# TensorE's four parts of a step in another order, the old maximum a step ahead on VectorE, and other signals for the gathers of Pool

## The chip, the cores and the metric

The kernel runs on one core of a Trainium2 chip. The metric is the device time of one launch in microseconds (us), the median of several launches. A profiled execution gives, beside its time, a record of every instruction of the five engines: TensorE (PE, its weight loads apart as PEld), VectorE (DVE), ScalarE (ACT), GpSimd (POOL) and SyncE (SP), which issues DMAs.

## What is computed

A graph of 6250 nodes with 64 channels and 200,000 edges, sorted by destination, goes through two graph layers. The change lies in the first one, an attention that is applied in two hops:

```
def agg(emb):
    a_input = jnp.concatenate([emb[head], emb[tail]], axis=-1)
    h = a_input @ fc_w.T + fc_b
    e = jnp.sum(h * rel_e, axis=-1)
    e = jnp.where(e > 0, e, LEAKY_SLOPE * e)
    m = jax.ops.segment_max(e, head, num_segments=N)
    ex = jnp.exp(e - m[head])
    denom = jax.ops.segment_sum(ex, head, num_segments=N)
    w = ex / denom[head]
    agg_emb = jax.ops.segment_sum(emb[tail] * w[:, None], head, num_segments=N)
    return agg_emb + emb
for _ in range(N_HOPS):        # N_HOPS = 2
    emb = agg(emb)
    emb = emb / jnp.maximum(jnp.sqrt(jnp.sum(emb * emb, axis=-1, keepdims=True)), EPS)
```

After it come a layer norm, a second layer (gather, matmul with a weight that a GRU cell makes, segment sum, relu) and another layer norm. None of that is touched.

## The kernel before

The edges of a hop are cut into groups of 512, four tiles of 128 edges, padded so that a group belongs to one block of nodes. A hop takes one step for each group (about 400 steps), and each group passes through nine stages, one stage a step: in step `i` an engine works on group `i`, on `i - 1`, up to `i - 8`. `pipelined` writes eight steps out (`u` is 0 to 7), and a hardware loop runs over these eights. At the edge of an eight TensorE and ScalarE load the block numbers of the next eight steps from SBUF into registers (L83).

What each engine does in step `i`, in the order of before:

- **TensorE**: `sums(i-7)` (L1553, the probability weighted sums of the gathered rows), `scores(i-2)` (L1540 and L1543, the products with the nodes' scores; the first three products on L1543 take a block number from a register), `spread(i-4)` (L1524, four transposes that lay the scores over all partitions), `turn_prob(i-6)` (L1532, four transposes of the probabilities), `gather(i-1)` (L1504, one product with zeros that opens `ps_t`, then L1515, ten matmul records that fetch rows near the diagonal out of SBUF by one-hot products). The sweep loop in `gather` runs once a step here. Each part ends with a semaphore: `summed`, `x_rdy`, `s_spread`, `p_turned`, `gathered`.
- **ScalarE**: `prob` (L1579, out of `ps_p` once `p_turned` is told), `prob_t` (L1584), `alpha` (L1586), `acc` (L1591), `rows<-ps_t` (L1599, once `gathered` is told; its signal is `kept`), `lower` (L1603). `ps_t` has one buffer: the next gather's L1504 waits for `kept`.
- **VectorE**: `m_old` (L1625), `x_sum` (L1633), `masked` with the new maximum `m_new` (L1642), `s_raw` (L1649), `hot_t` (L1654), `score` (L1660), `hot_near` (L1669, waits for `gathered` of two groups back), `block_sum` (L1677, waits for `summed`).
- **Pool**: for each group two indirect DMAs (L1486) that gather the far rows of the group's last two tiles from HBM into `rows`. The first waits for `summed` of the group that last held the slot, the second for `p_turned` of group `g - 7`.
- **SyncE**: two broadcast loads a step and one load of indices every four steps.

## Time and profile before

| | us |
|---|---|
| median of 3 runs (5886.37 to 5901.3) | 5893.11 |
| the profiled execution | 5902.71 |
| its span (first to last instruction) | 5900.9 |

The page's line of TensorE's busy tenths over 40 slices of the span reads 3666666199999999996799999999974666666664. The two stretches of nines are the two hops. The mean granted clock over the span is 0.846 of full speed. By queue, the hardware DMA queue q1 moved 799.51 MB and Pool's queue q0 147.90 MB.

How such rows are read: a row of the timeline has the start (us from the span's start), the duration, engine, line, operation, what it writes and reads, the number of merged records, and in brackets how long the engine was idle before it and who ended that. Ends of matmuls are modelled. A releaser "issue" means that the engine waited for nothing that the profile shows.

### The profile page before, as it was taken

The page shows a single profiled execution, that of the slowest core. Times are in us where ns is not written, and L with a number is a line of the kernel's source. Part 1 is how long each engine was busy: PE and PEld are TensorE (multiplying, and loading weights), DVE is VectorE, ACT ScalarE, POOL GpSimd, SP SyncE. Part 2 cuts the span into 40 slices and gives each one's busy share as a digit, 9 for nine tenths or more (in the row PEclk, how much of TensorE's full clock was granted, in tenths as well). Part 3 has the DMA queues.
Part 4 walks back from the last instruction along what each step waited for, and adds up shares of the span by engine and source line. Part 5 has one row for each costly group of instructions (what it writes and reads, how often), then busy time and mean ns, then how long its engine had stood idle before and what let it go on. Part 6 is the DMA issues. An engine that isn't in the chain of part 4 may idle for free. (4 is left out here: it accounts for less than half of the span.)

```text
span 5900.9 us, 199689 instructions
## 1 busy us (share of the span) xinstructions
PE 4518.9 (77%) x53517; PEld 3713.5 (63%) x53518; DVE 3763.9 (64%) x11123; ACT 2406.1 (41%) x5659; POOL 2851.1 (48%) x2835
## 2 busy tenths in 40 slices
PE   3666666199999999996799999999974666666664
PEld 0001111098899898986798989999973555555553
DVE  8984887377777777777577777777773333333334
ACT  6201000066666666664466666666650111111111
POOL 0155666245555555552455555555532555555553
PEclk7668887599999999998899999999985766666666
DMA  7999999355555555553555555555531222222221
GB/s 284 404 413 410 413 415 415 109 146 144 145 150 145 145 150 146 144 149 69 143 150 147 146 148 147 148 147 149 147 84 42 50 50 50 50 49 51 50 50 39
DMA packets 489464, 949.05 MB, mean 161 GB/s; under 512 B 146548, under 2 KB 295693, under 8 KB 440209
## 3 DMA queue, kind: packets, MB, share of 16 engines
q1 hardware_dynamic: 397953, 799.51, 41.9%
q0 software_dynamic: 90336, 147.90, 11.2%
q8 instruction: 60, 0.98, 0.1%
q10 hardware_dynamic: 1072, 0.31, 0.0%
q14 instruction: 43, 0.35, 0.0%
HBM read 930.99 MB, written 14.32 MB: 160 GB/s over the span
## 5 line engine op out<-in xcount | busy, mean ns | idle before, releaser
L1486 POOL DMA_INDIRECT rows<-tab_d,stage_idx x1632 | 1611.4, 987 | 1620.2 <-PE ps_p L1532 592.7
L1515 PE MATMUL ps_t<-tab,hot_near 128*128 x8160 | 1146.7, 287 | 55.8 <-issue 27.4
L1868 POOL DMA_INDIRECT tab<-y_d,stage_src x768 | 727.7, 947 | 735.3 <-PE ps_all L1909 276.2
L1515 PEld LDWEIGHTS ps_t<-tab,hot_near 128*128 128x128 f32 x8160 | 1006.5, 193 | 105.5 <-issue 91.5
L1553 PE MATMUL ps_g<-rows,prob 128*128 128x65 f32 x6528 | 846.6, 273 | 171.1 <-issue 97.0
L1553 PEld LDWEIGHTS ps_g<-rows,prob 128*128 128x128 f32 x6528 | 793.8, 192 | 209.6 <-issue 165.7
L595 PE MATMUL ps_gate<-ring,h_sb 128*1 128x512 f32 x3072 | 561.2, 815 | 381.0 <-DMA ring<-w_ih 174.2
L1960 DVE TENSOR_SCALAR to_node<-wins_list,row_all 128x384 bf16<-128x384 bf16 x864 | 262.5, 324 | 865.4 <-remote 440.9
L1579 ACT ACTIVATE prob<-ps_p 128x512 f32<-128x512 f32 x816 | 486.9, 597 | 798.4 <-PE ps_p L1532 653.6
L1669 DVE TENSOR_SCALAR hot_near<-arena,node_code 128x640 f32<-128x640 bf16 x816 | 463.6, 568 | 400.8 <-PE ps_t L1515 254.3
L2022 ACT ACTIVATE arena<-ps_all 128x384 bf16<-128x384 f32 x432 | 211.7, 490 | 1172.3 <-PE ps_all L1896 531.3
L1642 DVE CUSTOM_DVE_ANT_0 masked<-lower,ps_s,m_old 128x512 f32<-128x512 bf16 x816 | 609.9, 747 | 26.6 <-PE ps_s L1524 7.4
L1909 PE MATMUL ps_all<-arena,to_node 128*128 128x64 bf16 x7776 | 499.1, 223 | 134.3 <-issue 85.3
L1603 ACT ACTIVATE lower<-arena,far_bias 128x512 bf16<-128x512 bf16 x816 | 582.2, 713 | 0.0
L1584 ACT ACTIVATE prob_t<-masked,m_new 128x512 f32<-128x512 f32 x816 | 581.6, 713 | 0.4 <-DVE m_new L1642 0.3
L532 POOL DMA_INDIRECT rec_d<-arena,row_all x294 | 336.5, 1144 | 486.6 <-PE ps_gate L595 435.9
L1909 PEld LDWEIGHTS ps_all<-arena,to_node 128*128 128x128 bf16 x7776 | 414.4, 114 | 225.0 <-issue 171.2
L1524 PE MATMUL ps_s<-ident_f,score 128*128 128x128 f32 x3264 | 517.1, 281 | 0.8 <-issue 0.8
L1532 PE MATMUL ps_p<-ident_f,prob_t 128*128 128x128 f32 x3264 | 493.2, 274 | 3.2 <-issue 2.8
L595 PEld LDWEIGHTS ps_gate<-ring,h_sb 128*1 128x1 f32 x3072 | 41.3, 81 | 710.8 <-DMA ring<-w_ih 410.5
L1599 ACT ACTIVATE rows<-ps_t 128x230 f32<-128x230 f32 x816 | 289.5, 355 | 406.0 <-PE ps_t L1515 329.4
L1543 PE MATMUL ps_x<-a_split,hot_t 128*128 x9792 | 443.6, 184 | 11.8 <-issue 11.7
(456 smaller groups left out, 6896.0 us busy)
## 6 DMA issues: line engine op xcount, KB each, us to landing
arena<-lo_d SPq DMA_DIRECT2D x816, 256.0 KB
ring<-w_ih SPq DMA_DIRECT2D x192, 1024.0 KB
ring<-w_hh SPq DMA_DIRECT2D x192, 1024.0 KB
arena<-code_d SPq DMA_DIRECT2D x816, 160.0 KB
arena<-list_lo_d SPq DMA_DIRECT2D x216, 128.0 KB
rows<-tab_d,stage_idx POOLq DMA_INDIRECT x1632
tab<-y_d,stage_src POOLq DMA_INDIRECT x768
rec_d<-arena,row_all POOLq DMA_INDIRECT x294
```

The costliest lines, as they stand in the source:

```text
L595: mm = pe.matmul(ps_gate[32 * j:32 * j + 1, r % 2, :], lhsT=h_sb[:, pc:pc + 1], rhs=ring[:, n % RING, j, :], start=(pc == 0), stop=(pc == ...
L1486: pool.indirect_dma_start(out=rows[:, h * 4 + g, k, :], out_offset=None, in_=tab_d[hop], in_offset=bass.IndirectOffsetOnAxis(ap=stage_idx[ ...
L1515: mm = pe.matmul(ps_t[:, k * TW:(k + 1) * TW], lhsT=hot_near[:, p, at0 + b, :], rhs=tab[:, ds(at + b, 1), 0:TW].rearrange("p a c -> p (a c)"),
L1524: mm = pe.transpose(ps_s[:, p, k * P:(k + 1) * P], score[:, p, k:k + 1].broadcast_to([P, P]), ident_f[:])
L1532: mm = pe.transpose(ps_p[:, k * P:(k + 1) * P], prob_t[:, p, k * P:(k + 1) * P], ident_f[:])
L1553: mm = pe.matmul(ps_g[:, p, 0:C + 1], lhsT=prob[:, p, k * P:(k + 1) * P], rhs=rows[:, u, k, 0:C + 1], start=(k == 0), stop=(k == KT - 1))
L1579: act.activation(prob[:, q, :], ps_p[:], ACT.Copy).then_inc(prob_rdy, 1)
L1584: act.activation(prob_t[:, q, :], masked[:, q, :], ACT.Exp, bias=m_new[:, q:q + 1], scale=-1.0)
L1603: act.activation(lower[:, (u - 1) % 4, :].rearrange("p (k e) -> p k e", k=KT), lo_wide[:, (u - 1) % 8].rearrange("p (k s e) -> p k s e", k ...
L1642: dve.tensor_tensor_reduce(masked[:, p, :], lower[:, (u - 5) % 4, :], ps_s[:, p, :], 1.0, m_old[:, p:p + 1], ALU.add, ALU.min, m_new[:, p: ...
L1868: pool.indirect_dma_start(out=rows[:, g, k].rearrange("p j c -> p (j c)"), out_offset=None, in_=y_d, in_offset=bass.IndirectOffsetOnAxis(a ...
L1909: mm = pe.matmul(ps_total[:, ds(slots[j % KT] + k, 1), :].rearrange("p a c -> p (a c)"), lhsT=to_node[:, j % 4, k * P:(k + 1) * P], rhs=go ...
```

## The change

1. TensorE: `sums` moves from the first to the third place, behind `scores` and `spread`. Its operands and waits are as they were.
2. VectorE: `m_old` of group `g` is made in step `g + 4`, behind `s_raw`, and no longer in step `g + 5` ahead of `x_sum`. It gets four slots for two. The waits that others imply are left out in steps in which all stages run.
3. Pool: the first DMA of a group waits for `p_turned` of group `g - 7` (the second did), the second for `x_rdy` of group `g - 2`, that is for `scores` in TensorE's next step.

```
-                m_old = sbh("m_old", [P, 2])
+                m_old = sbh("m_old", [P, 4])
...
                                 for k in range(NEAR, KT):
-                                    if k == KT - 1:
+                                    if k == NEAR:
                                         wait_tick(pool, tick, p_turned, g0 + g - 6)
+                                    else:
+                                        wait_tick(pool, tick, x_rdy, g0 + g - 1)
...
                         def body(i, u, stages, number):
-                            if stages[7]:
-                                sums(i - 7, (u - 7) % 2, (u - 7) % 8)
                             if stages[2]:
                                 scores(i - 2, u % 2, (u - 2) % 8, number(1))
                             if stages[4]:
                                 spread(i - 4, u % 2)
+                            if stages[7]:
+                                sums(i - 7, (u - 7) % 2, (u - 7) % 8)
                             if stages[6]:
                                 turn_prob(i - 6, u % 2)
...
-                                act.activation(alpha[:, (u - 5) % 4:(u - 5) % 4 + 1], m_old[:, q:q + 1], ACT.Exp,
+                                act.activation(alpha[:, (u - 5) % 4:(u - 5) % 4 + 1], m_old[:, (u - 5) % 4:(u - 5) % 4 + 1], ACT.Exp,
...
-                            if stages[5]:
-                                g, p = i - 5, (u - 5) % 2
-                                wait(dve, exp_rdy, g - 1)
-                                wait(dve, masked_rdy, g)
-                                link.mark(dve.tensor_tensor(m_old[:, p:p + 1], m_new[:, 1 - p:2 - p], m_cap[:, ds(g, 1)], ALU.max))
-                                old_at = link.base + link.n
...
+                            if stages[4]:
+                                g, p, r = i - 4, (u - 4) % 2, (u - 4) % 4
+                                if not steady:
+                                    wait(dve, exp_rdy, g - 3)
+                                wait(dve, masked_rdy, g)
+                                link.mark(dve.tensor_tensor(m_old[:, r:r + 1], m_new[:, 1 - p:2 - p], m_cap[:, ds(g, 1)], ALU.max))
```

TensorE at the edge of an eight in hop 1, before: the loop's branch, the load of the block numbers, then the first part of the next step.

```order
L112 ISA
L112 COMPARE_AND_BRANCH
L83 ISA
L83 TENSOR_LOAD first_b
L38 ISA
L38 REGISTER_ALU [waits landed1_0]
L1553 MATMUL ps_g<-rows,prob 128x65 [waits added_0,prob_rdy_0]
L1553 MATMUL ps_g<-rows,prob 128x65 x3
```

The same place after (its lines are numbered 2 higher there).

```order
L112 ISA
L112 COMPARE_AND_BRANCH
L83 ISA
L83 TENSOR_LOAD first_b
L38 REGISTER_ALU
L38 REGISTER_ALU [waits hot_t_rdy_0]
L1542 MATMUL ps_x<-far_type,hot_t 128x50 [waits score_rdy_0]
L1545 REGISTER_ALU x2
L1545 ISA
L1545 MATMUL ps_x<-a_split,hot_t 128x50
L1545 ISA
L1545 MATMUL ps_x<-a_split,hot_t 128x50
```

What moved: the part that needs no block number no longer stands between the load of the numbers (and, in the other seven steps, the gather's own register work) and the register instructions of `scores`.

Pool inside the loop of hop 1, before.

```order
L1486 DMA rows<-tab_d,stage_idx 128x128 [waits summed_0]
L45 REGISTER_ALU
L1486 DMA rows<-tab_d,stage_idx 128x128 [waits p_turned_0]
```

Pool at the same place after.

```order
L1488 DMA rows<-tab_d,stage_idx 128x128 [waits summed_0,p_turned_0]
L45 REGISTER_ALU
L1488 DMA rows<-tab_d,stage_idx 128x128 [waits x_rdy_0]
```

What moved: no instruction, but the signal for each DMA comes from a later part of TensorE's work.

VectorE, one step of the written-out eight, before.

```order
L1677 SCALAR_TENSOR_TENSOR block_sum<-block_sum,alpha,ps_g 128x65 [waits kept_0]
L1625 ISA [waits masked_rdy_0,exp_rdy_0]
L1625 TENSOR_TENSOR m_old<-m_new,group_first 128x1
L1633 TENSOR_TENSOR x_sum<-ps_x,rows 128x200 [waits x_rdy_0,landed3_0,kept_0]
L1640 REGISTER_ALU [waits s_spread_0,lower_rdy_0]
L1642 ISA masked,m_new<-lower,ps_s,m_old 128x512 [waits dvh_0]
L1642 ISA m_new 128x1
L1647 REGISTER_ALU
L1649 TENSOR_REDUCE s_raw<-x_sum 128x4 [waits dvh_0]
L1654 TENSOR_SCALAR hot_t<-arena,part_f 128x1024 [waits x_rdy_0,lo_in1_0]
```

VectorE, the same step after.

```order
L1683 SCALAR_TENSOR_TENSOR block_sum<-block_sum,alpha,ps_g 128x65 [waits kept_0]
L1630 TENSOR_TENSOR x_sum<-ps_x,rows 128x200 [waits x_rdy_0,landed3_0]
L1641 ISA masked,m_new<-lower,ps_s,m_old 128x512 [waits s_spread_0]
L1641 ISA m_new 128x1
L1645 REGISTER_ALU
L1647 TENSOR_REDUCE s_raw<-x_sum 128x4 [waits dvh_0]
L1653 ISA [waits masked_rdy_0]
L1653 TENSOR_TENSOR m_old<-m_new,group_first 128x1
L1659 TENSOR_SCALAR hot_t<-arena,part_f 128x1024
```

What moved: `m_old` from ahead of `x_sum` to behind `s_raw`, and six waits are gone.

## Rows read from the trace of the kernel before

**Rows 1.** Windows: length, busy PE, PEld, DVE, ACT, POOL, clock, DMA share, GB/s.
```profile
1190.00:2640.00 1450.00, 1347.47 (x16374) 1304.38 (x16375) 1068.19 (x3424) 931.37 (x2283) 753.78 (x761) 1.00 0.55 147
2860.00:4388.00 1528.00, 1421.64 (x17287) 1378.96 (x17287) 1124.47 (x3619) 984.76 (x2421) 784.49 (x797) 1.00 0.56 145
```

**Rows 2.** Groups of instructions: sums in hop 1, then in hop 2 (busy us, mean ns | idle us before).
```profile
L1553 PE MATMUL ps_g<-rows,prob 128*128 128x65 f32 x3048 | 394.7, 272 | 78.6 <-issue 45.5 <-ACT prob L1579 32.9
...
L1553 PE MATMUL ps_g<-rows,prob 128*128 128x65 f32 x3236 | 420.1, 273 | 83.0 <-issue 43.7 <-ACT prob L1579 38.9
```

**Rows 3.** Waits of TensorE in the same two stretches: us in total, times, longest.
```profile
PE ps_g L1553 <- ACT prob L1579: 32.9, 33, 1.4
...
PE ps_g L1553 <- ACT prob L1579: 38.9, 39, 1.4
```

**Rows 4.** Timeline: two neighbouring starts of L1504 at 1516, one step apart.
```profile
1516.84 0.17 PE L1504 MATMUL ps_t<-zero_t 128*128 128x1 bf16 x1
...
1520.21 0.17 PE L1504 MATMUL ps_t<-zero_t 128*128 128x1 bf16 x1
```

**Rows 5.** Timeline from 1505 to 1510, a step whose gather is told late.
```profile
1505.67 0.94 POOL L1486 DMA_INDIRECT rows<-tab_d,stage_idx  x1 [1.48 <-PE ps_g L1553]
...
1505.92 1.45 PE L1515 MATMUL ps_t<-tab,hot_near 128*128 x10
...
1506.92 0.94 POOL L1486 DMA_INDIRECT rows<-tab_d,stage_idx  x1 [0.30 <-issue]
...
1508.53 0.36 ACT L1599 ACTIVATE rows<-ps_t 128x230 f32<-128x230 f32 x1 [1.11 <-PE ps_t L1515]
...
1509.61 0.52 PEld L1515 LDWEIGHTS ps_t<-tab,hot_near 128*128 128x128 f32 x4 [0.24 <-issue]
```

**Rows 6.** Timeline at 1566, a step with one Pool transfer near its gather.
```profile
1565.67 0.94 POOL L1486 DMA_INDIRECT rows<-tab_d,stage_idx  x1 [1.11 <-issue]
...
1566.06 1.35 PE L1515 MATMUL ps_t<-tab,hot_near 128*128 x10
...
1567.67 0.35 ACT L1599 ACTIVATE rows<-ps_t 128x230 f32<-128x230 f32 x1
```

**Rows 7.** Waits of all engines from 1500 to 2300 us, 210 steps.
```profile
ACT rows L1599 <- PE ps_t L1515: 72.7, 88, 1.4
DVE hot_near L1669 <- PE ps_t L1515: 69.1, 89, 1.4
```

**Rows 8.** Timeline behind an edge, 1529 to 1534.
```profile
1529.44 0.95 POOL L1486 DMA_INDIRECT rows<-tab_d,stage_idx  x1 [0.30 <-issue]
...
1530.27 0.19 PE L1540 MATMUL ps_x<-far_type,hot_t 128*128 128x50 bf16 x1
...
1530.68 0.63 PE L1524 MATMUL ps_s<-ident_f,score 128*128 128x128 f32 x4
1531.14 0.60 PE L1532 MATMUL ps_p<-ident_f,prob_t 128*128 128x128 f32 x4
1531.21 0.94 POOL L1486 DMA_INDIRECT rows<-tab_d,stage_idx  x1 [0.83 <-issue]
...
1532.93 0.60 ACT L1579 ACTIVATE prob<-ps_p 128x512 f32<-128x512 f32 x1 [2.94 <-PE ps_p L1532]
...
1533.61 0.94 POOL L1486 DMA_INDIRECT rows<-tab_d,stage_idx  x1 [1.45 <-PE ps_p L1532]
...
1533.77 0.43 PE L1553 MATMUL ps_g<-rows,prob 128*128 128x65 f32 x2 [0.81 <-ACT prob L1579]
```

**Rows 9.** Timeline at 1187, the last step of hop 1 without sums: scores behind gather.
```profile
1187.44 0.19 PE L1540 MATMUL ps_x<-far_type,hot_t 128*128 128x50 bf16 x1
1187.62 0.36 PEld L1543 LDWEIGHTS ps_x<-a_split,hot_t 128*128 128x128 bf16 x3 [0.18 <-issue]
...
1188.24 0.63 PE L1524 MATMUL ps_s<-ident_f,score 128*128 128x128 f32 x4
```

More of the change, by code:

```diff
@@ L1619, in body @@
                         def body(i, u, stages, _):
-                            if stages[5]:
-                                g, p = i - 5, (u - 5) % 2
-                                wait(dve, exp_rdy, g - 1)
-                                wait(dve, masked_rdy, g)
-                                link.mark(dve.tensor_tensor(m_old[:, p:p + 1], m_new[:, 1 - p:2 - p], m_cap[:, ds(g, 1)], ALU.max))
-                                old_at = link.base + link.n
+                            steady = all(stages)
                             if stages[3]:
-                                g, q = i - 3, (u - 3) % 2
-                                wait(dve, kept, g + 1)
-                                v = (u - 3) % 8
+                                g, q, v = i - 3, (u - 3) % 2, (u - 3) % 8
+                                if not steady:
+                                    wait(dve, kept, g + 1)
                                 wait(dve, landed[v], (g - v) * ((KT - NEAR) * 2) + (KT - NEAR) * 16)
@@ L1633, in body @@
                                 link.mark(dve.tensor_tensor(x_sum[:], ps_x[:, q, 0:KT * R].rearrange("p (k r) -> p k r", k=KT),
-                                                            rows[:, (u - 3) % 8, :, SC:SC + R], ALU.add))
+                                                            rows[:, v, :, SC:SC + R], ALU.add))
                                 sum_at = link.base + link.n
                             if stages[5]:
-                                g, p = i - 5, (u - 5) % 2
-                                wait(dve, lower_rdy, g + 1)
+                                g, p, r = i - 5, (u - 5) % 2, (u - 5) % 4
+                                if not steady:
+                                    wait(dve, exp_rdy, g - 1)
+                                    wait(dve, lower_rdy, g + 1)
+                                    link.sync()
                                 wait(dve, s_spread, g + 1)
-                                dve.wait_ge(link.sem, old_at)
                                 dve.sem_inc(dtick, 1)
                                 dve.tensor_tensor_reduce(masked[:, p, :], lower[:, (u - 5) % 4, :],
-                                                         ps_s[:, p, :], 1.0, m_old[:, p:p + 1],
+                                                         ps_s[:, p, :], 1.0, m_old[:, r:r + 1],
                                                          ALU.add, ALU.min, m_new[:, p:p + 1]).then_inc(masked_rdy, 1)
                             if stages[3]:
-                                g, q = i - 3, (u - 3) % 2
                                 dve.wait_ge(link.sem, sum_at)
@@ L1649, in body @@
                                 link.mark(dve.tensor_reduce(s_raw[:, q, :], x_sum[:], AX, ALU.min))
+                            if stages[4]:
+                                g, p, r = i - 4, (u - 4) % 2, (u - 4) % 4
+                                if not steady:
+                                    wait(dve, exp_rdy, g - 3)
+                                wait(dve, masked_rdy, g)
+                                link.mark(dve.tensor_tensor(m_old[:, r:r + 1], m_new[:, 1 - p:2 - p], m_cap[:, ds(g, 1)], ALU.max))
                             if stages[1]:
                                 g = i - 1
-                                wait(dve, lo_in[(u - 1) % 2], rows_in(g, u - 1))
-                                wait(dve, x_rdy, g - 1)
+                                if not steady:
+                                    wait(dve, lo_in[(u - 1) % 2], rows_in(g, u - 1))
+                                    wait(dve, x_rdy, g - 1)
                                 dve.tensor_scalar(hot_t[:, (u - 1) % 2].rearrange("p k s e -> p (k s e)"), lo_wide[:, (u - 1) % 8, :],
@@ L1657, in body @@
                                 g, q = i - 3, (u - 3) % 2
-                                wait(dve, s_spread, g - 1)
+                                if not steady:
+                                    wait(dve, s_spread, g - 1)
                                 link.sync()
```

## The prediction

> **What bounds the kernel now.** I read the page first (slices, then the costliest groups), then the windows over the two hops, the groups and waits inside them, and last the timeline step by step. The windows show that over the 2978 us in which both hops run with all stages TensorE is busy 2769 us, 93%, while VectorE has 2193, ScalarE 1916 and Pool 1538 us [rows 1]. The granted clock is 1.00 in both, the 2.4 GHz level, so nothing in the sum is put down to the clock. A step has 8 records of the sums' matmuls, so 3048/8 + 3236/8 = 785 steps lie in these windows [rows 2], or 98 eights, at 2978/785 = 3.79 us each. An undisturbed step takes 1520.21 - 1516.84 = 3.37 us [rows 4], which I take as 3.38: TensorE then issues without a gap, and no new order of the same parts goes below it. What the change can touch is the excess, 2978 - 785 x 3.38 = 325 us. The reader is to see in it three pieces.
>
> First, TensorE waits for "issue" ahead of the sums for 45.5 + 43.7 = 89.2 us, 0.91 us at each of the 98 edges of an eight: the load of the block numbers with the branch [rows 2, 8]. Second, ahead of the same sums it waits for ScalarE's `prob`, 72 times, 71.8 us [rows 3]. One such wait: the transposes are issued at 1531.14 and modelled to end at 1531.74, but `prob` starts only at 1532.93 after 2.94 us of idling, and the sums at 1533.77, 0.81 us late [rows 8]. Third, the rest, 325 - 89 - 72 = 164 us, sits mostly in steps that last about 3.70, as the one from 1505.92 to 1509.61 does, with hardly an idle record on PE [rows 5].
>
> That third piece is a ring. The ten gather matmuls start at 1505.92 and are modelled to end at 1507.37; ScalarE's copy of `ps_t` has been idle 1.11 us for them and starts at 1508.53, 1.16 us past that end. The copy takes 0.36, then `kept` lets TensorE open the next gather, whose first weights load at 1509.61, 0.72 us past the copy's end, after 0.24 us idle [rows 5]. 1509.61 - 1505.92 = 3.69, the period. So the 1.16 us in which a finished gather isn't told sets these steps. Beside it stands what Pool does: two transfers 1.25 us apart (1505.67, 1506.92), the second across the gather's end. In another step there is one transfer at 1565.67 and none near it; the same ten matmuls end at 1567.41 and the copy starts at 1567.67, 0.26 us later [rows 6]. In 1500 to 2300 us ScalarE waits so for the gather 88 times of 210, VectorE 89 times, 0.8 us each [rows 7]. I read it as this: signals of TensorE that fall due while Pool works through a close pair of transfers come only when the second is through, about 1.6 us from its start (1508.53 - 1506.92). At 1531 the same: a transfer at 1531.21, and the transposes' signal shows at 1532.93, 1.72 us on [rows 8].
>
> **The Trainium skill on these ends.** By "Perfetto Trace Analysis", section "Summary: the profiler window per engine type", the reported end of a TensorE instruction is an estimate, and that of a software-generated DMA is the end of descriptor generation. By that rule the 1.16 us could be matmul time that the record leaves out; the sum would then lose the third piece, and the result be that of rival 3. The 0.26 us after the same ten matmuls [rows 6] speaks against it.
>
> **The change part by part.**
>
> *Sums behind scores and spread.* Scores take 1530.68 - 1530.27 = 0.41 us and spread 1531.14 - 1530.68 = 0.46 [rows 8], so some 0.85 us stand between the gather and the sums from now on. The wait for `prob` was 71.8/72 = 1.0 us on the mean; 0.85 us of it is covered at once, and the rest goes with the late signal that made it. I book -72. If the signals stay late, 0.15 x 72 = 11 us of it stay.
>
> The price is at the edge. Scores need five register instructions ahead of their first three `a_split` products. Behind the sums these are hidden, as those 0.41 us show. Directly behind a gather they aren't: 1188.24 - 1187.44 = 0.80 us, with TensorE's weight load idle 0.18 in front of the first of them alone [rows 9]. So 0.39 us more. At an edge nothing is queued ahead, so it is paid in full: 98 x 0.39 = +38 us. Inside an eight the question is whether TensorE's sequencer runs far enough ahead. The step of rows 9 had just come out of a late start of its gather. In a steady step the sums and the transposes (1.3 us of issue) now lie ahead of the gather's register work, for the 0.85 us of before, and the wait for `prob`, which held the sequencer up just behind the gather, is met by then. The bounds are 0 and 0.39 us a step; I take 0, since with a 1.3 us start the sequencer has three times 0.39 in hand. By "TensorE: Matmul & The Clock Gate", the table at the top, the engine's queue is 64 deep; by that rule such a lead has room, and the price inside an eight is 0; no run here shows the depth.
>
> *What waits for the sums.* VectorE's `block_sum` and Pool. `block_sum` now comes 0.85 us later in the step, and VectorE's next step begins behind it. VectorE has 2193/785 = 2.79 us of work a step against 3.38, and its products (`hot_t`, `hot_near`, `score`) are used one to two steps on. Cost 0 while the step is over some 3.1 us.
>
> *m_old and the waits.* `m_old` is the same instruction in another place, now ahead of `hot_t` and out of the path from `block_sum` to `x_sum` and `masked`; the waits left out had long been met. VectorE has the slack above, so both are booked at 0, with bounds of 0 and nothing below: no gain can come from an engine with half a microsecond to spare, except after an edge, where at most some 0.2 us x 98 = 20 us could be.
>
> *Pool.* A signal of the transposes that lets ScalarE start at 1532.93 lets Pool start at 1533.61, 0.68 us later [rows 8]; with the little by which the signal is older than ScalarE's start I take 0.8 us. In an undisturbed step counted from the end of the transposes at 0, the first transfer starts at 0.8, the gather ends at 1.35, scores at about 1.6 to 1.8, the second transfer starts at 2.4 to 2.6, the next transposes end at 3.38 and the next first transfer starts at 4.15. Distances 1.6 to 1.8 us both ways, in place of 1.25 and 2.45. The gather's end then falls 0.6 us behind the start of a lone transfer, and on this pattern is told at once, as at 1567, where it falls 1.74 us behind one. The rows have no pair at 1.6 to 1.8 that I would call steady (at 1529.44 and 1531.21, 1.77 apart, a signal was late), so I bound the third piece from both sides: all 164 us gone, or none. I take 60%, -98, for it also holds steps lengthened by other things (loads of indices, transfers that catch up). Later transfers cost nothing themselves: a group's rows are first read three steps after they are issued.
>
> **Sum.** -72 + 38 - 98 = -132 us. The profiled execution took 5902.7, 9.6 over the median of the runs. 5893 - 132 = 5761. With all of the third piece: 5893 - 72 + 38 - 164 = 5695. With none: 5859.
>
> **The rivals.**
>
> 1. *Scores pay in every step.* The sequencer finds no lead behind the gather, and 0.39 us is added 785 times. Even with all late signals gone the excess is 785 x 0.39 + 89 = 395 in place of 325: +70, 5963. It decides from 0.3 us a step. For it: rows 9 are the only steps of the trace in this order. Against: the longer queue ahead of the gather. 9%.
>
> 2. *The transfers pair up elsewhere.* Scores' signal is held by the first transfer, so the second starts late and runs close to the next first one, across the next gather's end. Then every step, not half of them, is a ring of 3.70: 785 x 0.32 + 89 + 38 = 378, +53, 5946. It decides where scores' signal comes over 0.4 us late. For it: the late signal at a distance of 1.77 us [rows 8]. Against: scores end before the point behind a transfer where that one fell due (over 1.0 us). 13%.
>
> 3. *Only the wait for prob goes* (the gather is told as late as now, whatever makes it so): -72 + 38 = -34, 5859. 14%.
>
> 4. *Nothing moves*, the gain at the sums being given back at the edges and at `block_sum`: 5893. 6%.
>
> **How the numbers follow.** My forecast, 5695 to 5830 with 5761 as its centre, has 58%. A measurement can tell about 0.3%, 18 us. Faster by more than that: the forecast and nearly all of rival 3, 0.72. Within it: rival 4 and the edge of rival 3, 0.09. Slower: rivals 1 and 2, 0.19. The range reaches from 5690 to 5950: it leaves out rival 1 and the little below 5690 that VectorE's 20 us could bring. As time I give 5760.
>
> **What would show it.** Right: waits of the sums for `prob` near 0; ScalarE's `rows` and VectorE's `hot_near` wait for the gather far fewer than 88 times in 210 steps; Pool's transfers 1.6 to 1.8 us apart; an issue wait of about 0.9 us 98 times, now ahead of scores, with another 0.4 inside scores; steps of 3.38 between. Wrong: an idle time of PEld ahead of L1543 records in most steps (rival 1); the `ps_t` wait of ScalarE in nearly all steps and Pool pairs at 1.25 us (rival 2). The forecast falls as a whole if the median step stays at 3.70 with Pool's transfers apart: then Pool wasn't what held the signals.

## The result, and the profile after

The changed kernel takes 6023.3 us in the median of four runs (6016.3 to 6024.6), the kernel before beside it 5894.2 us: a ratio of 1.0213, 95% interval 1.0201 to 1.0226. It is slower by 2.1%, where 5760 us was predicted. The profiled execution took 6024.6 us with a span of 6022.8; that of before 5902.7.

The same kernel before takes about 5286 us at some times and 5894 to 5983 us at others, two chips gave both, and so every ratio here is against the kernel before measured beside it. I call the first a prompt place and the second a late place, for a reason that the runs give below. The profile that the prediction worked with, and the result, are of the late kind.

The windows over the two hops after, which answer to [rows 1] (length, busy PE, PEld, DVE, ACT, POOL, granted clock, DMA share, GB/s):

```profile
1190.00:2640.00 1450.00, 1363.63 (x15739) 1289.68 (x15739) 976.85 (x3295) 907.33 (x2196) 703.36 (x733) 0.99 0.54 141
2860.00:4388.00 1528.00, 1422.31 (x16250) 1342.20 (x16251) 1014.08 (x3407) 937.59 (x2259) 726.55 (x763) 0.98 0.53 140
```

TensorE is as busy as before and has done 5% less work in the same stretch (15739 + 16250 matmul records against 16374 + 17287). The clock has a small part in it: it averages 0.99 and 0.98 where it was 1.00 in both windows. Over the whole of both hops the trace's granted clock was at its lower level, 1.2 GHz, for 72 us, and for 30 us before. At half the speed that is at most 36 - 15 = 21 us of the loss (my estimate). Where the rest is: the next rows are the sums' matmuls of each hop, 3264 to a hop, with the start of the first and of the last (name, count, shortest/median/longest ns, first to last start). Before:

```profile
L1553 PE MATMUL ps_g<-rows,prob x3264: 233/275/324, 1190.7 to 2735.0; 128*128 128x65 f32 x192
...
L1553 PE MATMUL ps_g<-rows,prob x3264: 233/275/444, 2852.9 to 4390.6; 128*128 128x65 f32 x192
```

After, with the list of what TensorE idled for ahead of them in the first hop:

```profile
L1555 PE MATMUL ps_g<-rows,prob x3264: 217/275/447, 1177.2 to 2783.0; 128*128 128x65 f32 x192
its engine sat idle before it (us, times) until:
  issue: 6.1, 10
...
L1555 PE MATMUL ps_g<-rows,prob x3264: 217/275/426, 2891.8 to 4514.7; 128*128 128x65 f32 x192
```

The hops went from 1544.3 and 1537.7 us to 1605.8 and 1622.9: +61.5 and +85.2, together +147. With 408 steps each, a step takes 3.94 and 3.98 us in place of 3.78 and 3.77. Outside the hops 25 us were won: the first sums come 13.5 us sooner, the stretch between the hops is 9 us shorter, the rest behind them 2 us. 147 - 25 = 122 us, the difference of the two profiled executions. The sums no longer wait for `prob` at all (72 waits in [rows 3]); so that wait went, as predicted, and something larger came.

The waits of all engines from 1500 to 2300 us after (line, releaser: us in all, times, longest), which answer to [rows 7]:

```profile
POOL rows L1488 <- PE ps_x L1545: 166.7, 96, 2.4
DVE block_sum L1683 <- PE ps_g L1555: 123.3, 133, 2.2
ACT rows L1601 <- PE ps_t L1517: 113.3, 136, 1.4
...
DVE hot_near L1675 <- PE ps_t L1517: 70.7, 117, 1.1
```

ScalarE's copy of the gather waits for it 136 times, in two steps of three, where it was 88 of 210 before. The timeline of two neighbouring steps after (start, us, engine, line; in brackets the idle time ahead and its releaser) answers to [rows 4] and [rows 5]:

```profile
1541.31 0.95 POOL L1488 DMA_INDIRECT rows<-tab_d,stage_idx  x1 [1.63 <-PE ps_x L1545]
...
1541.63 0.17 PE L1506 MATMUL ps_t<-zero_t 128*128 128x1 bf16 x1
1541.66 1.35 PE L1517 MATMUL ps_t<-tab,hot_near 128*128 x10
...
1542.58 0.95 POOL L1488 DMA_INDIRECT rows<-tab_d,stage_idx  x1 [0.32 <-issue]
...
1544.21 0.36 ACT L1601 ACTIVATE rows<-ps_t 128x230 f32<-128x230 f32 x1 [0.84 <-PE ps_t L1517]
...
1545.00 0.17 PE L1506 MATMUL ps_t<-zero_t 128*128 128x1 bf16 x1
1545.11 0.94 POOL L1488 DMA_INDIRECT rows<-tab_d,stage_idx  x1 [1.59 <-PE ps_g L1555]
...
1545.34 1.45 PE L1517 MATMUL ps_t<-tab,hot_near 128*128 x10 [0.17 <-issue]
...
1546.36 0.94 POOL L1488 DMA_INDIRECT rows<-tab_d,stage_idx  x1 [0.30 <-issue]
1546.66 0.18 PE L1542 MATMUL ps_x<-far_type,hot_t 128*128 128x50 bf16 x1
1546.97 0.35 PEld L1545 LDWEIGHTS ps_x<-a_split,hot_t 128*128 128x128 bf16 x3 [0.25 <-issue]
...
1547.57 0.63 PE L1526 MATMUL ps_s<-ident_f,score 128*128 128x128 f32 x4
...
1549.32 0.17 PE L1506 MATMUL ps_t<-zero_t 128*128 128x1 bf16 x1
```

The first step lasts 1545.00 - 1541.63 = 3.37 us, the floor. In it the gather is modelled to end at 1543.01 and the copy starts at 1544.21, 1.20 us later and 1.63 us behind the start of the second of two Pool transfers that are 1.27 us apart. The second step pays: its gather opens 0.31 us late (1545.34 - 1545.00 against 1541.66 - 1541.63), and scores, now directly behind it, take 1547.57 - 1546.66 = 0.91 us against 0.41 [rows 8], with the weight load of L1545 idle 0.25 in front of one product. Step two lasts 4.32 us. That is rival 2 with rival 1 on its back: Pool's pair now lies over the end of each gather, since the second transfer of a group waits for scores' signal (1.63 and 1.59 us idle), and the first of the next group follows at once behind it (0.32 and 0.30). The row at 1545.11 names the sums as what ended its wait, but the trace's semaphore events say otherwise. The signal of the scores that end at 1543.41 came at 1544.34, 0.93 us late, and Pool's wait for it ended there. The sums' signal came only at 1544.74, and it is the next transfer that waits for it.

### The profile page after: what moved, and what is told of

It is laid out like the page before. It is cut to its first block and busy times, and to the rows that moved or that the text cites. A ratio compares the mean times of both kernels' runs of the same rounds, so it can differ in the third digit from the quotient of the medians.

```text
span 6022.8 us, 197687 instructions
## 1 busy us (share of the span) xinstructions
PE 4683.2 (78%) x53517; PEld 3805.1 (63%) x53518; DVE 3660.4 (61%) x11123; ACT 2436.5 (40%) x5659; POOL 2808.8 (47%) x2835
## 5 line engine op out<-in xcount | busy, mean ns | idle before, releaser
L1488 POOL DMA_INDIRECT rows<-tab_d,stage_idx x1632 | 1559.8, 956 | 1798.4 <-PE ps_x L1545 788.6
L1555 PE MATMUL ps_g<-rows,prob 128*128 128x65 f32 x6528 | 828.2, 270 | 14.4 <-issue 14.0
L1915 PE MATMUL ps_all<-arena,to_node 128*128 128x64 bf16 x7776 | 512.2, 224 | 149.1 <-issue 114.5
L1683 DVE SCALAR_TENSOR_TENSOR block_sum<-block_sum,alpha,ps_g 128x65 f32<-128x65 f32 x816 | 230.4, 282 | 637.4 <-PE ps_g L1555 516.0
L1545 PE MATMUL ps_x<-a_split,hot_t 128*128 x9792 | 554.6, 186 | 53.4 <-issue 9.8
L1545 PEld LDWEIGHTS ps_x<-a_split,hot_t 128*128 128x128 bf16 x9792 | 441.0, 96 | 145.8 <-issue 107.3
L1542 PE MATMUL ps_x<-far_type,hot_t 128*128 128x50 bf16 x3264 | 448.1, 185 | 96.3 <-issue 87.4
```

The source lines that it names most:

```text
L1488: pool.indirect_dma_start(out=rows[:, h * 4 + g, k, :], out_offset=None, in_=tab_d[hop], in_offset=bass.IndirectOffsetOnAxis(ap=stage_idx[ ...
L1545: mm = pe.matmul(ps_x[:, p, k * R:(k + 1) * R], lhsT=hot_t[:, p, k, 0, :], rhs=a_split[:, ds(bb, 1), j, :].rearrange("p a r -> p (a r)"), ...
L1555: mm = pe.matmul(ps_g[:, p, 0:C + 1], lhsT=prob[:, p, k * P:(k + 1) * P], rhs=rows[:, u, k, 0:C + 1], start=(k == 0), stop=(k == KT - 1))
L1915: mm = pe.matmul(ps_total[:, ds(slots[j % KT] + k, 1), :].rearrange("p a c -> p (a c)"), lhsT=to_node[:, j % 4, k * P:(k + 1) * P], rhs=go ...
```

## Experiments

**The parts one by one.** Four kernels in a prompt place (5286.5 us before). The first has TensorE's order alone:

```diff
-                            if stages[7]:
-                                sums(i - 7, (u - 7) % 2, (u - 7) % 8)
                             if stages[2]:
                                 scores(i - 2, u % 2, (u - 2) % 8, number(1))
                             if stages[4]:
                                 spread(i - 4, u % 2)
+                            if stages[7]:
+                                sums(i - 7, (u - 7) % 2, (u - 7) % 8)
```

> The kernel before with TensorE's new order alone (sums behind scores and spread); Pool's waits and VectorE's order are as before. Theory A (Pool's new waits pair its transfers across the end of every gather, and TensorE's signals come late): without them this order loses nothing, the wait of the sums for prob (71.8 us) is gone and the edges cost 38 more: 5860, and not above 5900. Theory B (the register instructions of scores stand exposed behind the gather, about 0.5 us in the steps whose gather starts late): this part alone carries the loss, 5980 to 6030.

Measured: 5302.8 us, ratio 1.0027 (1.0017 to 1.0038).

The second has Pool's waits alone:

```diff
-                                    if k == KT - 1:
+                                    if k == NEAR:
                                         wait_tick(pool, tick, p_turned, g0 + g - 6)
+                                    else:
+                                        wait_tick(pool, tick, x_rdy, g0 + g - 1)
```

> The kernel before with Pool's new waits alone (first transfer behind the transposes, second behind scores). Theory A: in the old order scores come 0.9 us later, so the second transfer starts only about 1.2 us ahead of the next first one and the pair lies across the gather; slower than before, 5950 or more. Theory B: within 20 us of 5893.

Measured: 5286.2 us, 0.9995 (0.9986 to 1.0005).

The third has VectorE's part alone, with the four columns of `m_old`:

```diff
-                m_old = sbh("m_old", [P, 2])
+                m_old = sbh("m_old", [P, 4])
...
-                                link.mark(dve.tensor_tensor(m_old[:, p:p + 1], m_new[:, 1 - p:2 - p], m_cap[:, ds(g, 1)], ALU.max))
...
+                            if stages[4]:
+                                g, p, r = i - 4, (u - 4) % 2, (u - 4) % 4
...
+                                link.mark(dve.tensor_tensor(m_old[:, r:r + 1], m_new[:, 1 - p:2 - p], m_cap[:, ds(g, 1)], ALU.max))
```

> The kernel before with VectorE's part alone (the old maximum a step ahead, implied waits left out). Both theories: VectorE has half a microsecond of slack in each step, so 5875 to 5900, at most 20 us faster.

Measured: 5290.0 us, 1.0006 (0.9997 to 1.0016).

The fourth is the whole change with Pool's waits put back (the second diff undone):

> The changed kernel with Pool's waits put back. Theory A: the loss of 129 us is gone, 5840 to 5900. Theory B: it stays at 5980 to 6030, and VectorE's part changes nothing against TensorE's order alone.

Measured: 5305.7 us, 1.0033 (1.002 to 1.0045). What follows: here TensorE's order costs 0.3%, the other two parts nothing that can be told, and the loss of 2.1% isn't there. My expectations were made for steps of 3.7 us, and this place has none: in the third kernel's trace 199 of the 227 steps between 1500 and 2300 us take 3.38 us, and the other 28, 4.47 to 4.54 us, are those with an edge.

**The whole change again.** This is a late place (5982.7 us before).

> The changed kernel as it stands, beside the kernel before. On the chip of the first four experiments every part alone was within 0.35% of the kernel before (5286 us), while the kernel before itself took 5893 us where the change was measured. If the loss of 2.1% is a property of the parts together (theory A in the form that pairing needs both the new order and the new waits), it shows here too: ratio 1.02. If it needs the late signals of the place where it was measured (steps of 3.7 us in the kernel before, which the kernel before doesn't have at 5286 us), the ratio is that of TensorE's order alone, 1.003.

Measured: 6063.8 us in two runs, 1.0132 (1.0101 to 1.0162). The loss is there, with another size.

**Repeats and a kernel without transfers.** The next seven kernels were meant for a late place, and both places were prompt (5285.2 us before for the first four, 5288.6 for the last three). Two kinds of kernel are new. They leave Pool's transfers out of the loops; the first eight groups of rows stand for all, and the waits for a transfer become constants, as in this diff of the one made from before (the other is made from after in the same way):

```diff
-                            wait(pe, landed[u], (g - u) * ((KT - NEAR) * 2) + (KT - NEAR) * 16)
+                            wait(pe, landed[u], (KT - NEAR) * 16)
...
-                        with loop(pool, 1, pool_n) as it:
-                            for h in range(2):
-                                half(it, h)
```

> The changed kernel with Pool's waits put back, once more, meant for a chip on which the kernel before takes over 5800 us (there TensorE's signals come late). Theory A (Pool's new waits do the harm): on such a chip it is at or below the kernel before. Theory B (scores' register instructions exposed behind a gather that starts late): it stays 1 to 2% above the kernel before. On a chip where the kernel before takes 5286 us: 1.003 again.

> The kernel before with Pool's new waits alone, once more. On a chip with late signals: theory A 1 to 2% slower than before, theory B the same as before. On the other kind of chip: 1.000.

> The kernel before without Pool's transfers inside the loops of the hops: only the first eight groups are fetched, and later groups read those rows again, so the far rows of its sums and scores are not the right ones. If a pair of transfers is what holds TensorE's signals back, then on a chip with late signals the steps fall to 3.38 us and the hops lose all but the edges of their excess: some 250 us less than the kernel before. If the matmuls themselves are slower on such a chip, the steps stay at 3.7 to 3.8 and the time within 50 us of before. On the other kind of chip nothing changes, 5286.

> The changed kernel without Pool's transfers inside the loops of the hops (far rows as in the run of the kernel before without them). If the transfers hold the signals: the same as the kernel before without them to within 15 us (the edges cost 12 to 38 us more, the wait for prob is gone). If scores' register instructions are the loss by themselves, it is 100 us or more above it.

> The changed kernel with Pool's waits put back, meant for a chip with late signals (kernel before over 5800 us). Theory A (Pool's new waits do the harm): at or below the kernel before. Theory B (scores' register instructions, exposed behind a gather that starts late): 1 to 2% above it. Where the kernel before takes 5286 us: 1.004.

> The kernel before with Pool's new waits alone. On a chip with late signals: theory A 1 to 2% slower, theory B the same as before. On the other kind of chip 1.000.

> The changed kernel without Pool's transfers inside the loops of the hops, so its far rows are those of the first eight groups. On a chip with late signals: if the transfers hold the signals, the hops run at 3.38 us a step and the whole is 300 to 400 us below the changed kernel. If the chip's matmuls or register loads are slow by themselves, less than 100 us are gained. On the other kind of chip 5295.

Measured, in this order: 1.0039 (1.0024 to 1.0053), 0.9999 (0.9989 to 1.0008), 0.9987 (0.9977 to 0.9997), 1.0018 (1.0008 to 1.0027), 1.0034 (1.0022 to 1.0047), 0.9999 (0.9989 to 1.0009), 1.0020 (1.001 to 1.003). In a prompt place the transfers cost almost nothing: without them the kernel before gains 0.13%, the changed one some 0.15% (1.0018 and 1.0020 here against the 1.0034 of the whole change in the next experiment). So Pool's transfers alone don't make a place late.

**The whole change beside Pool's waits undone.** A prompt place again (5285.9 us before).

> The whole change, beside a run with Pool's old waits on the same chip. Two kinds of chip have shown themselves: the kernel before takes about 5286 us on one and 5893 to 5983 us on the other, where TensorE's signals come late around Pool's transfers. If the kernel before takes about 5286 us here: the theory (late signals carry the loss, and a quick chip has none) expects what TensorE's order alone cost, 5303 to 5308 us (ratio 1.003 to 1.004); the rival (Pool's new distances cost time by themselves as soon as TensorE's order is new as well) expects more, 5340 us or above (1.01). If the kernel before takes about 5900 us here: both expect 1.013 to 1.022, as in the two runs of the whole change so far, with steps of 3.4 and 4.3 us in turn.

> The change with Pool's waits put back as they were. If the kernel before takes about 5900 us here: the theory (Pool's new waits set its transfers in pairs across the end of each gather, and these hold TensorE's signals) expects the loss to be gone, ratio 0.995 to 1.005; the rival (TensorE's order makes the loss on such a chip by itself, since it moves the gather and its signal closer to any pair of transfers) expects 1.012 to 1.022 here too, the same as with the whole change. If the kernel before takes about 5286 us: 1.003 to 1.004 by both, as three runs have shown.

Measured: 5301.3 us, 1.0034 (1.0020 to 1.0048), and 5301.9 us, 1.0032 (1.0019 to 1.0045). So in a prompt place the whole change costs what TensorE's order alone does. The sums of the two hops with the whole change there:

```profile
L1555 PE MATMUL ps_g<-rows,prob x3264: 222/275/448, 1173.9 to 2610.5; 128*128 128x65 f32 x192
...
L1555 PE MATMUL ps_g<-rows,prob x3264: 222/275/447, 2717.4 to 4153.1; 128*128 128x65 f32 x192
```

and with TensorE's order as before and Pool's new waits (e2), also prompt:

```profile
L1555 PE MATMUL ps_g<-rows,prob x3264: 233/275/446, 1177.6 to 2608.8; 128*128 128x65 f32 x192
...
L1555 PE MATMUL ps_g<-rows,prob x3264: 233/275/448, 2716.4 to 4147.2; 128*128 128x65 f32 x192
```

1436.6 + 1435.7 against 1431.2 + 1430.8 us: +10.3, on 102 edges 0.10 us each. The timeline of the whole change there shows the edge behind a steady step:

```profile
1510.09 1.12 POOL L1488 DMA_INDIRECT rows<-tab_d,stage_idx  x1 [0.68 <-issue]
...
1511.84 0.94 POOL L1488 DMA_INDIRECT rows<-tab_d,stage_idx  x1 [0.63 <-issue]
...
1513.46 1.03 POOL L1488 DMA_INDIRECT rows<-tab_d,stage_idx  x1 [0.68 <-issue]
...
1514.27 0.17 PE L1506 MATMUL ps_t<-zero_t 128*128 128x1 bf16 x1
...
1516.15 0.19 PE L1542 MATMUL ps_x<-far_type,hot_t 128*128 128x50 bf16 x1 [0.51 <-issue]
...
1517.10 0.63 PE L1526 MATMUL ps_s<-ident_f,score 128*128 128x128 f32 x4
...
1518.85 0.17 PE L1506 MATMUL ps_t<-zero_t 128*128 128x1 bf16 x1
```

Pool's transfers are 1.75 and 1.62 us apart, what the prediction forecast, and the edge step takes 4.58 us: 0.51 idle ahead of scores and 1517.10 - 1516.15 = 0.95 in them, 0.54 over the 0.41 of [rows 8]. The idle time ahead of the edge shrank from the 0.91 of before (0.89 in e2) to 0.5 us, so most of the register work in scores was bought back there.

**Pool's waits undone in a late place** (5982.1 us before).

> The change with Pool's waits put back, sent alone, for the case that it meets a chip of the late kind (where the kernel before takes about 5900 us). There the theory (Pool's new waits make the pairs that hold TensorE's signals) expects a ratio of 0.990 to 1.005 and no steps of 4.3 us in turn with 3.4; the rival (TensorE's order is enough for the loss) expects 1.012 to 1.022. Where the kernel before takes about 5286 us, both expect 1.003 to 1.004.

Measured: 6027.2 us, 1.0075 (1.0056 to 1.0094). Neither side had this: there is a loss, and it is smaller than with the whole change (1.0132, with 5982.7 us before). Its timeline, one step:

```profile
1544.73 0.94 POOL L1486 DMA_INDIRECT rows<-tab_d,stage_idx  x1 [1.49 <-PE ps_p L1532]
...
1545.97 0.95 POOL L1486 DMA_INDIRECT rows<-tab_d,stage_idx  x1 [0.31 <-issue]
...
1546.50 0.61 PE L1532 MATMUL ps_p<-ident_f,prob_t 128*128 128x128 f32 x4
...
1547.94 0.60 ACT L1579 ACTIVATE prob<-ps_p 128x512 f32<-128x512 f32 x1 [1.51 <-PE ps_p L1532]
...
1548.16 0.19 PE L1540 MATMUL ps_x<-far_type,hot_t 128*128 128x50 bf16 x1
...
1548.82 0.63 PE L1524 MATMUL ps_s<-ident_f,score 128*128 128x128 f32 x4
```

The pair is 1.24 us apart here too, but it falls on the transposes: they end at 1547.11 and `prob` starts at 1547.94, 1.97 us behind the second transfer. Scores take 0.66 us, 0.25 more than before. So the old waits hold another signal of the same step, and the step pays a little less. By the semaphore events from 1500 to 2300 us the transposes' signal is over 0.3 us late in 164 of 204 steps and the gather's in 2 of 184; in the result's trace it is 13 of 121 and 135 of 167 (not every event was recorded).

**Without transfers, and Pool's waits alone, in a late place** (5898.9 us before).

> The change, with Pool's transfers left out of the loops over the groups of both hops: only the first eight groups of rows are fetched, the groups behind them read what lies there (so the output isn't the reference's), and no step waits for a transfer. If the kernel before takes about 5980 us here: the theory (Pool's transfers are what TensorE's signals are held behind) expects steps of 3.38 us but for one of 4.6 in eight, mean 3.54 as where the kernel before takes 5286 us, so 785 x (3.80 - 3.54) = about 200 us off the kernel before: 5780 us, ratio 0.96 to 0.97. The rival (something else in such a place holds them, whatever Pool does) expects steps of 3.9 to 4.0 us and 1.007 to 1.015. If the kernel before takes about 5286 us: 1.002, as twice before.

> Pool's new waits alone, TensorE's and VectorE's order as before. If the kernel before takes about 5980 us here: the theory that the two parts cost apart (TensorE's order 0.75% as in e15, Pool's waits the other 0.6% of the whole change) expects 1.004 to 1.008; the rival (what costs is how Pool's pairs meet the gather's end in TensorE's new order) expects 0.997 to 1.002 with TensorE's old order. If the kernel before takes about 5286 us: 1.000, as three times before.

Measured without transfers: 5666.5 us, 0.9611 (0.9592 to 0.9630), where 0.96 to 0.97 was expected if the transfers hold the signals. (The expectation was made for 5980 us before; with 5899 its 200 us give the same ratio.) Its sums:

```profile
L1552 PE MATMUL ps_g<-rows,prob x3264: 222/275/447, 1179.5 to 2614.0; 128*128 128x65 f32 x192
...
L1552 PE MATMUL ps_g<-rows,prob x3264: 222/275/296, 2719.9 to 4153.9; 128*128 128x65 f32 x192
```

1434.5 and 1434.0 us: the hops run as in a prompt place, 3.52 us a step, and the list of waits from 1500 to 2300 us no longer has a wait for the gather:

```profile
ACT prob L1578 <- PE ps_p L1531: 257.0, 227, 2.3
DVE block_sum L1680 <- PE ps_g L1552: 136.0, 226, 1.3
DVE hot_near L1672 <- issue: 60.6, 227, 0.3
```

Measured for Pool's waits alone: 5914.5 us, 1.0027 (1.0014 to 1.0040). It lies between what the two theories expected (for about 5980 us before), and its interval reaches both, so it decides nothing. Its sums:

```profile
L1555 PE MATMUL ps_g<-rows,prob x3264: 233/275/422, 1177.0 to 2737.7; 128*128 128x65 f32 x192
...
L1555 PE MATMUL ps_g<-rows,prob x3264: 233/275/418, 2844.6 to 4407.2; 128*128 128x65 f32 x192
```

The hops take 1560.7 + 1562.6 us, 41 more than the trace of before, and 25 us are won outside them: the first sums at 1177.0 in place of 1190.7, 106.9 us in place of 117.9 between the hops. The changed kernel has the same 25, and the run with Pool's old waits (e15) starts its first sums at 1190.7 again. So that gain seems to be of Pool's waits, and only in late places: in prompt ones the first sums come at 1177.6 with the new waits (e2) and at 1175.3 with the old (e3).

**One transfer to a group, in a late place** (5977.2 us before). Of the two only the second is left, and the waits for what has landed count accordingly:

```diff
-                                for k in range(NEAR, KT):
-                                    if k == NEAR:
+                                for k in range(NEAR if isinstance(it, int) else KT - 1, KT):
+                                    if k == NEAR or not isinstance(it, int):
                                         wait_tick(pool, tick, p_turned, g0 + g - 6)
```

> The change with one of Pool's two transfers to a group left out in the loops over the groups of both hops (both for the first eight groups; so the output isn't the reference's), the one that is left released by the turned block. If the kernel before takes about 5900 to 5980 us here: the theory that two transfers close together hold TensorE's signals expects what e16 had without any transfer, steps of 3.38 us but one of 4.6 in eight (mean 3.53 to 3.55), ratio 0.960 to 0.966. The rival (each transfer holds them for itself) expects about half of what the pair costs, steps of 3.7 to 3.8 us, ratio 0.98 to 0.995. If the kernel before takes about 5286 us: 1.002 to 1.004.

Measured: 5696.3 us, 0.9531 (0.9514 to 0.9548). That is below the range of either theory, since the range was worked out from e16, where the kernel before takes 5899 and not 5977 us. The steps tell more than the ratio:

```profile
L1555 PE MATMUL ps_g<-rows,prob x3264: 222/275/447, 1178.2 to 2615.8; 128*128 128x65 f32 x192
...
L1555 PE MATMUL ps_g<-rows,prob x3264: 222/275/296, 2721.8 to 4158.8; 128*128 128x65 f32 x192
```

1437.6 and 1437.0 us, 3.52 us a step, with one transfer in each:

```profile
1502.25 1.35 PE L1517 MATMUL ps_t<-tab,hot_near 128*128 x10
...
1503.17 0.95 POOL L1488 DMA_INDIRECT rows<-tab_d,stage_idx  x1 [2.39 <-PE ps_p L1534]
...
1503.86 0.35 ACT L1601 ACTIVATE rows<-ps_t 128x230 f32<-128x230 f32 x1
...
1505.59 0.17 PE L1506 MATMUL ps_t<-zero_t 128*128 128x1 bf16 x1
...
1506.54 0.95 POOL L1488 DMA_INDIRECT rows<-tab_d,stage_idx  x1 [2.43 <-PE ps_p L1534]
```

So a lone transfer at this spot of the step costs nothing, and two that are 1.25 us apart cost 0.4 us a step. Whether it is their closeness, their number, or the rows that they move, this run doesn't separate, for it changes all three. The gather that ends at 1503.60, 0.43 us behind the transfer's start, is copied at once. Yet a lone transfer isn't without effect: by the semaphore events of this trace the signal of the scores of 1503.43 to 1504.00 came at 1504.65, 0.65 us late and 1.48 us behind the transfer's start (1.50 and 1.73 in the steps beside it). It is over 0.3 us late in 195 of 227 steps between 1500 and 2300 us. VectorE only uses it after `block_sum`, so nothing is late for it.

## Why the prediction was wrong

**The reading of the trace was right in its mechanism.** Signals of TensorE are held around Pool's transfers: with no transfers (e16) or one (e18) the late-told gathers are gone and the steps fall to 3.52 us on the mean, in a late place. The semaphore events of the traces, from 1500 to 2300 us, show it directly. Scores' signal is over 0.3 us late in 98 of 201 steps before and in 176 of 202 after; in e16 it is so in none of 227, and in a prompt place (e13), with all the transfers, in none of 225. Whether Pool's work on a transfer holds a signal or the movement of the rows does, no run separates: e16 leaves both out. The prediction set beside this the rule of the Trainium skill, "Perfetto Trace Analysis", section "Summary: the profiler window per engine type", that the ends of matmuls are estimates, by which the 1.16 us would be time of the matmuls. In e16 the copy never waits for the same ten matmuls, and each recorded signal of theirs comes within 0.01 us of their modelled end, so here it was not that.

**The wait for prob, -72.** Right in its place: idle time ahead of the sums is 6.1 us in the first hop, none of it for `prob`. But it was itself the child of a late signal. In a prompt place there is no trace of the kernel before, but e3, which has its order on TensorE and its waits on Pool, shows no such wait, and there the change has nothing to win.

**The edges, +38.** The term was 0.39 us each on top of an idle time of 0.91 that stays. In a prompt place the idle time shrinks to 0.50 and the price is 0.10 us an edge, +10 us in the hops (+15 in the whole). In the late place of the result TensorE still idles 0.93 us ahead of scores at an edge (42.6 us, 46 times in the window of the first hop), and scores there take 0.91 us (mean of 25 edges), 0.50 over 0.41. So nothing is bought back, and 102 edges pay about 51 us. The sign of the term was right in both. In e16, late but without transfers, the idle time is 0.51 us (14.3 us, 28 times): it too goes with the transfers.

**Pool, -98: the first of two steps that failed.** The forecast had the transfers 1.6 to 1.8 us apart, with the second released by scores' signal about a microsecond behind the first. In a prompt place they are (1.75, 1.62). The prediction's own reading was that signals are late only by *close* pairs, and so it counted scores' signal as prompt. By e18 a lone transfer holds exactly that signal, to 1.48 us behind its start, and in the trace of the result it came 0.93 us late. Pool then starts the second transfer late, has the first of the next group already released (0.30 us idle, "issue"), and the two run 1.27 us apart over the end of the next gather. This is rival 2, which had its point of decision at "over 0.4 us late"; e18 has 1504.65 - 1504.00 = 0.65. I had given it 13% on the argument that scores end nearer to their transfer's start than the late signal of [rows 8], which I put at over 1.0 us. The rows say otherwise: the transposes end at 1531.74, 0.53 us behind the transfer at 1531.21, so that argument had nothing under it. And that a lone transfer holds nothing was read from one whose gather ended 1.74 us behind it [rows 6], later than the 1.45 to 1.53 us at which most of e18's late signals of scores came. Nothing of the -98 came: ScalarE waits for the gather 136 times in place of 88.

**Scores' register work inside an eight, 0: the second step that failed, and the larger.** Rival 2's price of +53 was too small, as rival 1 was folded into it; measured +147 in the hops. The bound of 0 holds in a prompt place: steps of 3.37 there, with scores as short as ever. The prediction counted on 1.3 us of lead for TensorE's sequencer, since the wait for `prob` would be met; it left out the wait for `kept`, which stands ahead of the gather. The bound fails where `kept` comes late: then scores take 0.91 us, 0.50 more, nearly each second step. The prediction held rivals 1 and 2 to be alternatives; a late `kept` is what turns rival 1 on. In the result the gather's late signal makes it so, in e15 the late `prob`, which ScalarE works off ahead of the copy. The sentence on the Trainium skill's queue of 64 entries ("TensorE: Matmul & The Clock Gate", the table at the top) would have made the price 0; a deep queue doesn't help while TensorE's sequencer is itself held up by the wait in front of the gather. The wait is that for `kept`, and the trace has its end: in the step at the floor it is over at 1540.08, 1.55 us ahead of the gather's first product (L1506), in the long one at 1544.66, 0.34 us ahead. From 1500 to 2300 us, edges left out, scores take over 0.55 us in all 65 steps in which this lead is under 0.8 us, and in 5 of the 89 in which it is 1.2 us or more. That is a connection in one trace; no run moved the wait alone. It takes TensorE's new order: in the late places with the old one (before and e17) scores take 0.41 us in all steps of that stretch but one each.

**The sum again, for the hops of the result** (my estimate, from its trace). Scores inside an eight take 0.66 us on the mean, 0.25 over 0.41: in 714 steps +178. The edges are +51, the wait for `prob` -74 (34.6 and 38.9 us over the whole of both hops), Pool nothing. That is +155 for +147 measured. Against the forecast of -132 the two profiled executions differ by +122, that is by 254 us: 178 of scores inside an eight, 98 of Pool that didn't come, 13 of the edges, less the 25 won outside the hops, make 264. So in microseconds most of the loss is rival 1's, and Pool's late signals are what switched it on.

**VectorE, 0.** Nothing measurable alone in a prompt place (1.0006). `block_sum` waits for the sums more often, 123.3 us in 133 waits against 50.3 in 96 before, and the steps at 3.37 us have room for it. Alone in a late place it wasn't run.

**The sum of parts in late places.** Where before takes 5982 us, TensorE's order with VectorE's part costs +0.75% and all together +1.32%. Where it takes 5894 to 5899 us, Pool's waits alone cost +0.27% and all together +2.13%. No place has all three, so whether the parts add up isn't known. The hops of the changed kernel are nearly the same in both (3228.7 us in the trace of the result, 3239.4 in e5's), so most of the difference between +1.3% and +2.1% probably lies in the kernel before; which of its steps are better off in the second place is open, as there is no trace of before from a 5982 us place.

## What to carry to other kernels

A release that hangs on the signal of one engine and is delayed by what it releases is a loop: before moving a wait, ask not only when its signal falls due but what the operation that it lets go does to the next signal. A gain read from a trace with late signals is a gain in that state alone, so measure the kernel before at several times and on several chips before trusting a few per cent. And two rivals of a prediction may be one: ask whether the first switches the second on.

None of the complete kernels beat the one before in either kind of place. e18 shows where something may lie: with one transfer to a group rather than two it took 281 us less than before in a late place (5977.2 - 5696.3), but it also moves only half of these rows. How much one transfer of all of them would keep wasn't tried. In a prompt place there is little to win, since leaving out all transfers gave 0.13%.

## What the runs showed of the hardware

The kind of place was unexpected. The kernel before took 5286 us on one chip and later 5982 us on the same one; another had 5285 and 5899 us. The mean granted clock over the span tells the two apart: 0.84 to 0.85 in every late run, 0.90 in the prompt ones. Until the hops both are alike within some 17 us (first sums at 1173.9 to 1190.7). In the hops the difference is the held signals, 3.78 against 3.52 us a step. Behind the hops it is larger still: the run without transfers in the hops (e16, late place) and the whole change in a prompt place (e13) have hops of equal length, and the stretch from the last sums to the end is 1510.8 us in one and 1144.9 in the other. The windows over it, late first (length, busy PE, PEld, DVE, ACT, POOL, granted clock, DMA share, GB/s):

```profile
4160.00:5664.00 1504.00, 936.03 (x13405) 758.85 (x13405) 562.22 (x1944) 220.78 (x451) 730.57 (x768) 0.64 0.22 47
```

and prompt:

```profile
4160.00:5298.00 1138.00, 826.80 (x13404) 656.35 (x13405) 592.55 (x1944) 220.74 (x451) 732.66 (x768) 0.84 0.30 62
```

The same instructions, the same 731 to 733 us of Pool in 768 transfers, and a granted clock of 0.64 against 0.84: TensorE waits more, and its matmuls take 13% longer in sum. Signals held behind these transfers may be what starts that too; it wasn't tried. What makes a place late is open: the same kernel before ran in both kinds.
